# Mamba-2 block and ternary FFN on eight cores: the causal mask of the scan moves into PSUM, and three jobs leave VectorE

## The chip, the cores and the metric

The kernel runs on all 8 cores of one Trainium2 chip. Each core takes one half of the sequence of one of four batch rows. The cores don't wait for one another in the program. The metric is the device time in microseconds (us) of the slowest core.

## What is computed

The input has 4 rows of 2048 tokens with 2048 features. One layer is a Mamba-2 mixer and a feed-forward part with ternary weights, each with a residual and a LayerNorm. The core of the reference, shortened:

```
proj = hidden_states @ in_proj_w.T               # gate 4096, hbc 4352, dt 64
hbc = silu(conv4(hbc) + conv_b)                  # hs 4096, B 128, C 128
dt = softplus(dt + dt_bias);  A = -exp(A_log)    # 64 heads
step: state = state*exp(dt*A) + dt * x (outer) B;  y = state . C
y = (y + D*hs) * silu(gate);  y = rmsnorm(y) @ out_proj_w.T
x = layernorm(x + y)
x = layernorm(x + ffn(x))     # 8-bit rounded input, sign() weights, silu(g)*u, W_d
```

The kernel doesn't step through the tokens. For a tile of 128 tokens and a head with running sums a of dt*A it forms the matrix exp(a_t - a_s + ln dt_s) for all pairs of tokens s <= t, multiplies it by B_s.C_t, and multiplies that by x. What comes from earlier tiles is carried in a state of 128 x 4096.

## The kernel before

A small scheduler in Python (class `Prog`) takes the operations in the order in which they are written, puts each on the queue of its engine, and adds the semaphore waits that its lists of read and written names ask for. An engine runs its queue strictly in order, so the order of the code is the order of the work. The name of a buffer is the unit of a dependency: whoever writes `S32` waits for everybody who has read `S32` before. A dependency on an earlier operation of the same engine is a wait as well (except on TensorE).

The stages, with the places in the profiled span where they begin:

1. Projection and convolution of the previous half sequence, and its scan for the state at the end (`phase_a(False)`, `b1_pass`), from 0 us.
2. The same projection for the core's own 1024 tokens (`phase_a(True)`), and `scan_prep(True)`, which forms dt, a (`ahat`) and ln dt (`lndt`), and writes six arrays (high and low bf16 parts of a, -a and ln dt) to `flat_dram`, until about 1551 us.
3. The scan proper: a loop over 8 tiles `tt` of 128 tokens (lines 628 to 722), from 1600.7 to about 2720 us. This is where the change lies.
4. Output projection, LayerNorm, the FFN in two halves, the last LayerNorm.

A tile `tt` of the scan has these parts, in the order of the code:

- SyncE loads 8 panels of gate values into `sg_v` (L630). ScalarE applies Silu to all 4096 columns (L633, with a load of its function table before it). VectorE copies the state `S32` (f32, 4096 columns) to `Sbf` in bf16 (L635), so that the old state is there while the state is updated.
- `state_chunk` updates the state in 8 groups of 512 columns: L585, L594 and L596 on VectorE with matmuls L582, L588 and L591 between them. L596 writes `S32`.
- `g0rep`: one matmul for B_s.C_t (L637), which VectorE multiplies by the 0/1 mask `mask01` (L640), and three copies of the 128 columns beside it (L643), so that it serves four heads at once.
- 16 groups `hg` of four heads, in pairs. Each group: four matmuls with 6 rows each give the exponents of four heads (L650, `dmm`), VectorE cuts them off at 30 (L655, `dmin`), ScalarE takes the exponential (L657, `eexp`), VectorE multiplies by `g0rep` (L659, `ghat`), and four matmuls multiply by x (L664, `yi`). `dmatL` and `dmatR` hold the six rows.
- After the second group of a pair: the part of the old state (L671 from `Sbf`, L674), ScalarE brings one factor out of PSUM (L677, `eaev`), VectorE multiplies and adds (L678, L679 `yadd`), GpSimd has formed D*x in `hsd` (L680, `dhs`), VectorE adds it (L683, `yadd2`) and multiplies by the gate (L684, `ygate`), and ScalarE sums the squares (L687).
- RMSNorm, and the transposition of the tile by matmuls with the identity (L712, L719).

A pair thus handles 8 heads, and there are 8 pairs per tile and 64 in the scan. The groups share `DMIN` and are written one after the other; the matmuls of the second group stand behind `yi` of the first one on TensorE.

Of the kernel before, what the change touches and what calls it, by code (L numbers as in the profile page):

```python
# [174 lines left out]
def build_nc(taps=()):  # L175
    taps = set(taps)
    nc = bass.Bass("TRN2", target_bir_lowering=False)
    p = Prog()
# [38 lines left out]
    flat_dram = nc.dram_tensor("flat_dram", [NTT, 6, 64, 128], BF16, kind="Internal").ap()  # L217
# [22 lines left out]
    lndt = sb("lndt", [128, 512], F32)  # L240
# [25 lines left out]
    wsp = cv(AR5, 10240, 512, F32)  # L266
# [10 lines left out]
    y1 = cv(AR5, 12288, 512, F32)  # L277
    t_m = cv(AR5, 14336, 512, F32)
    ea_g = cv(AR5, 16384, 512, BF16)
    g0rep = cv(AR5, 17408, 512, BF16)  # L280
    ghat_v = [cv(AR5, 18432, 512, BF16), cv(AR5, 19456, 512, BF16)]
    dmin_v = cv(AR5, 20480, 512, F32)
# [37 lines left out]
    p.dma("sync", lambda g: g.dma_start(out=cumut[:], in_=cumut_d), ["d"], ["cumut"])  # L320
    p.dma("gpsimd", lambda g: g.dma_start(out=mask01[:], in_=cumut_d), ["d"], ["mask01"])
    p.dma("sync", lambda g: g.dma_start(out=selm[:], in_=selm_d), ["d"], ["selm"])
    p.dma("sync", lambda g: g.dma_start(out=convb_sb[:], in_=convb_d), ["d"], ["convb"])
# [163 lines left out]
    def scan_prep(full):  # L487
# [19 lines left out]
      p.v(lambda v: v.tensor_add(wsp[:], wsp[:], lndt[:]), ["wsp", "lndt"], ["wsp"])  # L507
      p.s(lambda s: s.activation(wsb_bf[:], wsp[:], AF.Exp), ["wsp"], ["wsb_bf"])
      p.s(lambda s: s.activation(lam_row[:], arow[:], AF.Exp), ["arow"], ["lam_row"])
      ea_tmp = cv(AR5, 8192, 512, BF16)  # L510
# [57 lines left out]
    def load_delta(tt):  # L568
        p.dma("sync", lambda g, tt=tt: g.dma_start(
            out=dmatL[0:2, :].rearrange("a (h t) -> a h t", h=64),  # L570
            in_=flat_dram[tt, 2:4]), [f"fl{tt}_2", f"fl{tt}_3", "dmatL"], ["dmatL"], tag="dlL")
        p.dma("sync", lambda g, tt=tt: g.dma_start(
            out=dmatL[4:6, :].rearrange("a (h t) -> a h t", h=64),
            in_=flat_dram[tt, 4:6]), [f"fl{tt}_4", f"fl{tt}_5", "dmatL"], ["dmatL"], tag="dlL")
        p.dma("sync", lambda g, tt=tt: g.dma_start(
            out=dmatR[2:4, :].rearrange("a (h t) -> a h t", h=64),
            in_=flat_dram[tt, 0:2]), [f"fl{tt}_0", f"fl{tt}_1", "dmatR"], ["dmatR"], tag="drL")

# [49 lines left out]
    for tt in range(NTT):  # L628
        for pan in range(8):
# [12 lines left out]
        for q in range(1, 4):  # L642
            p.v(lambda v, q=q: v.tensor_copy(g0rep[:, q * 128:(q + 1) * 128], g0rep[:, 0:128]),  # L643
                ["G0R"], ["G0R"], tag="g0rep")
        for hg in range(16):
            gb = hg % 2
            for j in range(4):
                h = hg * 4 + j
                p.t(lambda t, h=h, j=j, gb=gb:
                    t.matmul(pb[4 + gb][:, j * 128:(j + 1) * 128],  # L650
                             dmatL[0:6, h * 128:(h + 1) * 128],
                             dmatR[0:6, h * 128:(h + 1) * 128],
                             start=(j == 0), stop=(j == 3)),
                    ["dmatL", "dmatR"], [PB[4 + gb]], tag="dmm")
            p.v(lambda v, gb=gb: v.tensor_scalar_min(dmin_v[:], pb[4 + gb][:, :], 30.0),  # L655
                [PB[4 + gb], "DMIN"], ["DMIN"], tag="dmin")
            p.s(lambda s, gb=gb: s.activation(ghat_v[gb][:], dmin_v[:], AF.Exp),  # L657
                ["DMIN"], [f"GH{gb}"], tag="eexp")
            p.v(lambda v, gb=gb: v.tensor_mul(ghat_v[gb][:], ghat_v[gb][:], g0rep[:]),  # L659
# [9 lines left out]
            if hg % 2 == 1:  # L669
# [12 lines left out]
                       ["XT", "drep", "HSD"], ["HSD"], tag="dhs")  # L682
                p.v(lambda v: v.tensor_add(y1[:], y1[:], hsd[:]), ["y1", "HSD"], ["y1"], tag="yadd2")  # L683
                p.v(lambda v, g2=g_: v.tensor_mul(sg_v[:, g2 * 512:(g2 + 1) * 512], y1[:],  # L684
# [309 lines left out]
def _prep_shared(inputs):  # L994
# [23 lines left out]
    ident = np.eye(128, dtype=f32)  # L1018
    cumut = np.ascontiguousarray(np.triu(np.ones((128, 128), dtype=f32)))
    e01 = np.ascontiguousarray(np.kron(np.eye(64, dtype=f32), np.ones((1, 64), dtype=f32)))  # L1020
    return dict(wip=wip, convd=convd, convb=convb, wop=wop, wg=wg, wu=wu, wd=wd,
                dtb_t=dtb, alog_t=alog, d_row=drow, nw_t=nw_t,
                ident_in=ident, cumut_in=cumut, e01_in=e01)

# [34 lines left out]
```

How the kernel before makes its waits and increments, by code:

```python
            def run(eng):  # L158
                for op in per[ename]:
                    for (sk, v) in op.waits:
                        eng.wait_ge(sems[sk], v)
                    inst = op.fn(eng)
                    if op.milestone:
                        inst.then_inc(sems[op.semkey], 16 if op.is_dma else 1)
```

## Time and profile before

| | |
|---|---|
| median of 2 runs | 6089.91 us (6080.96 and 6098.87) |
| the profiled execution | 6059.51 us, span of its slowest core 6058.0 us |
| spans of the 8 cores in it | 5981.7 to 6058.0 us |
| granted TensorE clock, mean of a core | 0.761 to 0.767 of full speed |
| busy share of the span | TensorE 54%, VectorE 21%, ScalarE 16%, GpSimd 8% |
| scan (1600.7 to 2720 us) | TensorE busy 28%, VectorE 51%, ScalarE 19%, GpSimd 10% |

A time is in us from the first instruction of the core. Busy shares over the whole span mix stages with different limits, so the shares of the scan alone stand in the last line. In the rows, PE is TensorE, DVE is VectorE, ACT is ScalarE, POOL is GpSimd. AR stands for the arenas AR2 to AR5, in which most buffers lie, pb for a PSUM bank.

### The profile page before, as it was taken

How to read it: one execution, taken by the hardware profiler on the slowest of the kernel's cores; microseconds unless marked ns; L12 is line 12 of the kernel's file. 1: busy time of each engine (PE TensorE's matmuls, PEld its weight loads, DVE VectorE, ACT ScalarE, POOL GpSimd, SP SyncE). 2: the span in 40 equal slices, each digit the busy share in tenths (PEclk: the TensorE clock that was granted, in tenths of full speed). 3: DMA queues.
4: the chain of work that ended last, by engine and by line, in shares of the span. 5: the costliest groups of instructions: out<-in, count | busy, mean ns of one | idle time of the engine just before them, and what ended most of it. 6: DMA issues, size and time to landing. Idle time of an engine off the chain costs nothing.

```text
span 6058.0 us, 43938 instructions; the slowest of 8 cores (5981.7 to 6058.0 us)
## 1 busy us (share of the span) xinstructions
PE 3248.0 (54%) x15085; PEld 1332.9 (22%) x15085; DVE 1275.5 (21%) x2081; ACT 978.7 (16%) x1315; POOL 461.8 (8%) x620
## 2 busy tenths in 40 slices
PE   5884389884222222226541176767556767755540
PEld 2440034441011111112210032322222323322200
DVE  0114400111355555550006600000000000000003
ACT  1220011221011111110001122221112222111110
POOL 0000000000011110011110000001110000011100
PEclk9995589996555555558985588889888888888885
DMA  5530176440000000003332223332334233233323
GB/s 79 62 44 4 32 115 97 64 54 6 27 8 8 8 8 9 12 4 51 55 64 72 52 39 56 56 58 28 62 51 75 39 56 56 39 61 60 61 78 114
DMA packets 260287, 291.43 MB, mean 48 GB/s; under 512 B 52658, under 2 KB 237106, under 8 KB 257588
## 3 DMA queue, kind: packets, MB, share of 16 engines
q0 software_dynamic: 216096, 190.45, 23.7%
q1 hardware_dynamic: 43972, 98.17, 4.9%
q8 instruction: 125, 2.05, 0.1%
q14 instruction: 94, 0.77, 0.1%
HBM read 434.13 MB, written 44.83 MB: 79 GB/s over the span
## 4 chain that ended last, share of the span: by engine, by line
PE 43%; DMA 24%; DVE 16%; issue 8%; ACT 8%; DVEq 1%; SPq 0%; ACTq 0%; POOL 0%; POOLq 0%; another core or an unknown queue 0%
PE pb L410 8%; PE pb L874 7%; PE pb L869 7%; DMA AR<-wu 6%; DMA AR<-wd 6%; PE pb L899 5%; PE pb L380 4%; DMA AR<-wop 3%; DMA AR<-part_dram 3%; PE pb L741 2%; PE pb L421 2%; DMA AR<-wip 2%; DVE XT L719 1%; DVE AR L594 1%; DVE AR L585 1%
## 5 line engine op out<-in xcount | busy, mean ns | idle before, releaser
L869 PE MATMUL pb<-AR 128*128 128x512 bf16 x2048 | 813.7, 397 | 193.1 <-ACT AR L851 139.4
L874 PE MATMUL pb<-AR 128*128 128x512 bf16 x2048 | 812.6, 397 | 184.8 <-ACT AR L858 95.9
L899 PE MATMUL pb<-XT,AR 128*128 128x512 bf16 x2048 | 555.9, 426 | 409.6 <-ACT AR L895 328.6
L410 PE MATMUL pb<-AR 128*128 128x512 bf16 (+1 forms) x3264 | 511.4, 308 | 35.2 <-DMA AR<-wip 35.2
L899 PEld LDWEIGHTS pb<-XT,AR 128*128 128x128 bf16 x2048 | 205.8, 106 | 759.6 <-issue 610.2
L741 PE MATMUL pb<-AR,XT 128*128 128x512 bf16 x1024 | 258.2, 396 | 176.1 <-DMA AR<-wop 119.2
L880 DVE TENSOR_TENSOR XT<-pb,AR 128x512 bf16<-128x512 f32 x128 | 88.6, 692 | 1220.3 <-PE pb L869 1051.0
L410 PEld LDWEIGHTS pb<-AR 128*128 128x128 bf16 x3264 | 245.8, 97 | 299.1 <-issue 39.7
L664 PE MATMUL pb<-XT,AR 128*128 128x64 bf16 x512 | 47.6, 233 | 491.8 <-DVE AR L659 491.8
L869 PEld LDWEIGHTS pb<-AR 128*128 128x128 bf16 x2048 | 207.0, 101 | 463.5 <-issue 245.4
L874 PEld LDWEIGHTS pb<-AR 128*128 128x128 bf16 x2048 | 207.8, 101 | 458.8 <-issue 238.8
L452 DVE CAST XT<-pb 128x512 bf16<-128x512 f32 x128 | 88.5, 692 | 988.8 <-PE pb L447 971.1
L895 ACT ACTIVATE AR<-AR 128x512 bf16<-128x512 bf16 x256 | 160.8, 629 | 799.5 <-DMA AR<-wd 799.5
L380 PE MATMUL pb<-AR 128*128 128x512 bf16 x1024 | 223.2, 381 | 61.6 <-DMA AR<-wip 61.6
L588 PE MATMUL pb<-AR,BT 128*128 128x512 bf16 x128 | 75.0, 586 | 297.4 <-DVE AR L585 297.4
L878 ACT ACTIVATE AR<-pb 128x512 bf16<-128x512 f32 x128 | 76.4, 597 | 786.1 <-PE pb L869 786.1
L905 POOL DMA_DIRECT2D AR<-wd x240 | 126.8, 529 | 949.2 <-PE pb L899 891.0
L680 POOL TENSOR_TENSOR AR<-XT,AR 128x512 f32<-128x512 bf16 x64 | 115.7, 1808 | 1019.3 <-DVE AR L683 767.3
L416 ACT CAST AR<-pb 128x512 bf16<-128x512 f32 (+1 forms) x204 | 91.0, 446 | 537.1 <-PE pb L410 527.2
L741 PEld LDWEIGHTS pb<-AR,XT 128*128 128x128 bf16 x1024 | 95.0, 100 | 339.0 <-issue 255.0
L421 PE MATMUL pb<-AR 128*128 128x512 bf16 x544 | 130.1, 381 | 62.9 <-ACT AR L416 58.0
L664 PEld LDWEIGHTS pb<-XT,AR 128*128 128x128 bf16 x512 | 30.8, 117 | 522.1 <-issue 522.1
(194 smaller groups left out, 2931.6 us busy)
## 6 DMA issues: line engine op xcount, KB each, us to landing
AR<-wip POOLq DMA_DIRECT2D x26, 2048.0 KB, 19.2
AR<-wg POOLq DMA_DIRECT2D x32, 1024.0 KB, 13.9
AR<-wu POOLq DMA_DIRECT2D x32, 1024.0 KB, 20.3
AR<-wd POOLq DMA_DIRECT2D x256, 128.0 KB, 2.9
AR<-part_dram SPq DMA_DIRECT2D x48, 512.0 KB
AR<-wop POOLq DMA_DIRECT2D x128, 128.0 KB, 2.9
part_dram<-AR SPq DMA_DIRECT2D x32, 512.0 KB
AR<-convd POOLq DMA_DIRECT2D x68, 128.0 KB, 4.9
```

The lines of the kernel that those rows point to most:

```text
L380: t.matmul(pb[bank][:, :], x_fm_v[:, kc * TE + 3 + tt * 128: kc * TE + 3 + (tt + 1) * 128], wv[:, kc, :], start=(kc == 0), stop=(kc == NKC ...
L410: t.matmul(pb[bank][:, 0:j1 - j0], wv[:, kc, (oc - (pan - 8) * 4) * 128:(oc - (pan - 8) * 4 + 1) * 128], x_fm_v[:, kc * TE + j0: kc * TE + ...
L416: s.copy(hbc_v[:, slot * TE + j0: slot * TE + j1], pb[bank][:, 0:j1 - j0]),
L421: t.matmul(pb[bank][:, :], convd_v[cslot][:, k * 128:(k + 1) * 128], hbc_v[:, slot * TE + j0 + k: slot * TE + j0 + k + 512], start=(k == 0 ...
L680: p.pool(lambda g, tt=tt, g2=g_: g.tensor_mul(hsd[:], XT[:, tt * INTER + g2 * 512: tt * INTER + (g2 + 1) * 512], drep[:, g2 * 512:(g2 + 1) ...
L741: t.matmul(pb[tt][:, :], XT[:, tt * INTER + kc * 128: tt * INTER + (kc + 1) * 128], wopb[i][:], start=(kc == 0), stop=(kc == 31)),
L869: t.matmul(pb[jg][:, :], wgbr[:, kc, oc * 128:(oc + 1) * 128], xqTr[:, kc, jg * 512:(jg + 1) * 512], start=(kc == 0), stop=(kc == NKC - 1)),
L874: t.matmul(pb[2 + jg][:, :], wubr[:, kc, oc * 128:(oc + 1) * 128], xqTr[:, kc, jg * 512:(jg + 1) * 512], start=(kc == 0), stop=(kc == NKC ...
L880: p.v(lambda v, ho=ho, jg=jg: v.tensor_mul(p_fm[:, ho * T + jg * 512: ho * T + (jg + 1) * 512], pb[2 + jg][:, :], sgev[:]), [PB[2 + jg], " ...
L895: p.s(lambda s, i=i: s.sign(wdb[i][:], wdb[i][:]), [f"wdb{i}"], [f"wdb{i}"], tag="sgnD")
L899: t.matmul(pb[oc * 2 + jg][:, :], wdb[i][:, oc * 128:(oc + 1) * 128], p_fm[:, kci * T + jg * 512: kci * T + (jg + 1) * 512], start=(kci == ...
L905: p.dma("gpsimd", lambda g, opan=opan, Hhalf=Hhalf, nxt_k=nxt_k, i=i: g.dma_start(out=wdb[i][:], in_=wd_d[opan, Hhalf * 32 + nxt_k]), [f"w ...
```

## The change

It edits the scan at five places and adds two constants.

1. **The mask.** A fifth matmul is added to the PSUM bank of each group (`dmmtri`). It adds 30000 wherever s > t: `negid` is 30000 times the identity, and `slo4` is the strictly lower triangle of ones, four times side by side. The exponents are now formed with the opposite sign (the rows of `dmatL` and `dmatR` are loaded with a and -a exchanged, and `lndt` is negated in `scan_prep`), and ScalarE takes exp(-1 * value) straight out of PSUM. The cut at 30 on VectorE (`dmin`) goes.
2. **`Sbf`** is copied by ScalarE instead of VectorE, behind Silu of the gate.
3. **The three copies of `g0rep`** are made by ScalarE.
4. **`yadd2`**, the addition of D*x, is done by GpSimd.
5. **Constants**: two more DMAs on GpSimd's queue at the start (128 x 512 and 128 x 128, f32 in DRAM), and one small operation on VectorE in `scan_prep(True)`.

```diff
+    p.dma("gpsimd", lambda g: g.dma_start(out=slo4[:], in_=slo4_d), ["d"], ["slo4"])
+    p.dma("gpsimd", lambda g: g.dma_start(out=negid[:], in_=negid_d), ["d"], ["negid"])
...
+      if full:
+        p.v(lambda v: v.tensor_scalar(lndt[:], lndt[:], -1.0, None, ALU.mult),
+            ["lndt", "wsp"], ["lndt"], tag="negln")
...
-            in_=flat_dram[tt, 2:4]), [f"fl{tt}_2", f"fl{tt}_3", "dmatL"], ["dmatL"], tag="dlL")
+            in_=flat_dram[tt, 0:2]), [f"fl{tt}_0", f"fl{tt}_1", "dmatL"], ["dmatL"], tag="dlL")
...
-            in_=flat_dram[tt, 0:2]), [f"fl{tt}_0", f"fl{tt}_1", "dmatR"], ["dmatR"], tag="drL")
+            in_=flat_dram[tt, 2:4]), [f"fl{tt}_2", f"fl{tt}_3", "dmatR"], ["dmatR"], tag="drL")
...
-        p.v(lambda v: v.tensor_copy(Sbf[:], S32[:]), ["S32"], ["Sbf"], tag="sbf")
+        p.s(lambda s: s.copy(Sbf[:], S32[:]), ["S32"], ["Sbf"], tag="sbf")
...
-            p.v(lambda v, q=q: v.tensor_copy(g0rep[:, q * 128:(q + 1) * 128], g0rep[:, 0:128]),
+            p.s(lambda s, q=q: s.copy(g0rep[:, q * 128:(q + 1) * 128], g0rep[:, 0:128]),
...
-                             start=(j == 0), stop=(j == 3)),
+                             start=(j == 0), stop=False),
                     ["dmatL", "dmatR"], [PB[4 + gb]], tag="dmm")
-            p.v(lambda v, gb=gb: v.tensor_scalar_min(dmin_v[:], pb[4 + gb][:, :], 30.0),
-                [PB[4 + gb], "DMIN"], ["DMIN"], tag="dmin")
-            p.s(lambda s, gb=gb: s.activation(ghat_v[gb][:], dmin_v[:], AF.Exp),
-                ["DMIN"], [f"GH{gb}"], tag="eexp")
+            p.t(lambda t, gb=gb:
+                t.matmul(pb[4 + gb][:, :], negid[:], slo4[:], start=False, stop=True),
+                ["negid", "slo4"], [PB[4 + gb]], tag="dmmtri")
+            p.s(lambda s, gb=gb: s.activation(ghat_v[gb][:], pb[4 + gb][:, :], AF.Exp,
+                                              scale=-1.0),
+                [PB[4 + gb]], [f"GH{gb}"], tag="eexp")
...
-                p.v(lambda v: v.tensor_add(y1[:], y1[:], hsd[:]), ["y1", "HSD"], ["y1"], tag="yadd2")
+                p.pool(lambda g: g.tensor_add(y1[:], y1[:], hsd[:]), ["y1", "HSD"], ["y1"], tag="yadd2")
```

How the queues change is shown at three places. The line numbers of the changed kernel are larger by 2 to 11: L642 is Silu, L644 the copy to `Sbf`, L652 the `g0rep` copies, L659 `dmm`, L665 the mask matmul, L667 `eexp`, L670 `ghat`, L675 `yi`, L682 and L685 the matmuls of the old state, L688 `eaev`, L690 `yadd`, L691 `dhs`, L694 `yadd2`, L695 `ygate`, L698 the squares.

ScalarE at the start of the second tile, before:

```order
L633 ACTIVATE AR3<-AR3 128x4096 [waits sem_sync_d0,sem_sync_d1,sem_sync_d2,sem_sync_d3,sem_sync_d4,sem_sync_d5,sem_sync_d6,sem_sync_d7]
L657 ACTIVATE AR5<-AR5 128x512 [waits sem_vector] x2
L677 CAST AR5<-pb3 128x512 [waits sem_tensor]
L687 ACTIVATE AR5,sums8<-AR3 128x512 [waits sem_vector]
L657 ACTIVATE AR5<-AR5 128x512 [waits sem_vector] x2
```

ScalarE at the same place in the changed kernel:

```order
L642 ACTIVATE AR3<-AR3 128x4096 [waits sem_sync_d0,sem_sync_d1,sem_sync_d2,sem_sync_d3,sem_sync_d4,sem_sync_d5,sem_sync_d6,sem_sync_d7]
L644 CAST AR4<-AR4 128x4096
L652 COPY AR5<-AR5 128x128 [waits sem_vector]
L652 COPY AR5<-AR5 128x128 [waits sem_scalar] x2
L667 ACTIVATE AR5<-pb4 128x512 [waits sem_tensor]
L667 ACTIVATE AR5<-pb5 128x512 [waits sem_tensor]
L688 CAST AR5<-pb3 128x512 [waits sem_tensor]
L698 ACTIVATE AR5,sums8<-AR3 128x512 [waits sem_vector]
```

The copy L644 and the copies L652 now stand behind Silu and ahead of the first exponential, and the exponentials wait for TensorE instead of VectorE.

VectorE at the start of the second tile, before:

```order
L635 CAST AR4<-AR4 128x4096
L585 TENSOR_TENSOR AR4<-pb0,XT 128x512 [waits sem_tensor,sem_vector]
L594 TENSOR_TENSOR AR5<-AR4,pb2 128x512 [waits sem_tensor]
L596 TENSOR_TENSOR AR4<-AR5,pb1 128x512 [waits sem_vector]
L585 TENSOR_TENSOR AR4<-pb0,XT 128x512 [waits sem_tensor]
```

VectorE there in the changed kernel (the lines of `state_chunk` are larger by 9):

```order
L594 TENSOR_TENSOR AR4<-pb0,XT 128x512 [waits sem_tensor,sem_vector]
L603 TENSOR_TENSOR AR5<-AR4,pb2 128x512 [waits sem_tensor]
L605 TENSOR_TENSOR AR4<-AR5,pb1 128x512 [waits sem_scalar,sem_vector]
L594 TENSOR_TENSOR AR4<-pb0,XT 128x512 [waits sem_tensor]
L603 TENSOR_TENSOR AR5<-AR4,pb2 128x512 [waits sem_tensor,sem_vector]
```

The copy is gone from the head of the queue, and the first write of `S32` (L605) has a wait for ScalarE that it had not.

VectorE in the first pair of head groups of a tile, before:

```order
L655 TENSOR_SCALAR AR5<-pb4 128x512 [waits sem_tensor]
L659 TENSOR_TENSOR AR5<-AR5 128x512 [waits sem_scalar,sem_vector]
L655 TENSOR_SCALAR AR5<-pb5 128x512 [waits sem_tensor,sem_vector]
L659 TENSOR_TENSOR AR5<-AR5 128x512 [waits sem_scalar]
L678 TENSOR_TENSOR AR5<-pb7,AR5 128x512 [waits sem_scalar,sem_tensor]
L679 TENSOR_TENSOR AR5<-AR5,pb6 128x512 [waits sem_vector]
L683 TENSOR_TENSOR AR5<-AR5 128x512 [waits sem_gpsimd,sem_vector]
L684 TENSOR_TENSOR AR3<-AR5,AR3 128x512 [waits sem_vector]
```

VectorE there in the changed kernel:

```order
L670 TENSOR_TENSOR AR5<-AR5 128x512 [waits sem_scalar] x2
L689 TENSOR_TENSOR AR5<-pb7,AR5 128x512 [waits sem_scalar,sem_tensor]
L690 TENSOR_TENSOR AR5<-AR5,pb6 128x512 [waits sem_vector]
L695 TENSOR_TENSOR AR3<-AR5,AR3 128x512 [waits sem_gpsimd]
L670 TENSOR_TENSOR AR5<-AR5 128x512 [waits sem_scalar] x2
```

GpSimd's queue, which held only `dhs` (L680) in the scan, in the changed kernel:

```order
L691 TENSOR_TENSOR AR5<-XT,AR3 128x512 [waits sem_vector]
L694 TENSOR_TENSOR AR5<-AR5 128x512 [waits sem_gpsimd,sem_vector]
L691 TENSOR_TENSOR AR5<-XT,AR3 128x512 [waits sem_gpsimd]
L694 TENSOR_TENSOR AR5<-AR5 128x512 [waits sem_gpsimd,sem_vector]
L691 TENSOR_TENSOR AR5<-XT,AR3 128x512 [waits sem_gpsimd]
```

VectorE keeps five operations of a pair out of eight. `ygate` (L695) waits for GpSimd's addition (L694), and GpSimd's next `dhs` (L691) waits for the same addition.

TensorE in the first pair of the changed kernel; without the two L665 rows and with the old numbers it is the order of before:

```order
L659 MATMUL pb4<-AR2 128x128 x3
L665 MATMUL pb4<-slo4,negid 128x512
L675 MATMUL pb6<-XT,AR5 128x64 [waits sem_vector]
L675 MATMUL pb6<-XT,AR5 128x64 x3
L659 MATMUL pb5<-AR2 128x128 x4
L665 MATMUL pb5<-slo4,negid 128x512
```

## Rows read from the trace of the kernel before

**Rows 1.** Busy time by stage: PE, PEld, DVE, ACT, POOL; granted clock, DMA share, GB/s.
```profile
960.00:1340.00 380.00, 325.54 (x2022) 155.08 (x2020) 38.69 (x56) 85.53 (x156) 31.92 (x38) 1.00 0.48 65
1600.70:2720.00 1119.30, 314.56 (x1604) 122.64 (x1605) 572.25 (x1076) 211.52 (x360) 114.60 (x63) 0.50 0.03 8
```
**Rows 2.** The chain that ended last, in one pair: start us, us, what.
```profile
2364.40 0.70 DVE AR L683
```
**Rows 3.** One pair in time: start us, us, engine, line, operation [idle before <-releaser].
```profile
2354.75 0.69 DVE L684 TENSOR_TENSOR AR<-AR 128x512 bf16<-128x512 f32 x1
...
2355.54 0.63 ACT L687 ACTIVATE AR<-AR 128x512 f32<-128x512 bf16 x1 [3.34 <-DVE AR L684]
...
2356.17 0.61 ACT L657 ACTIVATE AR<-AR 128x512 bf16<-128x512 f32 x1
...
2357.76 0.60 PE L650 MATMUL pb<-AR 6*128 6x128 bf16 x4
2358.54 0.69 DVE L655 TENSOR_SCALAR AR<-pb 128x512 f32<-128x512 f32 x1 [1.23 <-PE pb L650]
2359.32 0.63 ACT L657 ACTIVATE AR<-AR 128x512 bf16<-128x512 f32 x1 [2.54 <-DVE AR L655]
2360.05 0.43 DVE L659 TENSOR_TENSOR AR<-AR 128x512 bf16<-128x512 bf16 x1 [0.82 <-ACT AR L657]
...
2360.81 0.61 PE L671 MATMUL pb<-AR,C_fm 128*128 128x512 bf16 x1
2361.36 0.60 PE L674 MATMUL pb<-AR,ea_fm 64*128 64x512 bf16 x1
...
2362.05 0.59 ACT L677 CAST AR<-pb 128x512 bf16<-128x512 f32 x1 [2.10 <-PE pb L674]
...
2363.61 0.69 DVE L679 TENSOR_TENSOR AR<-AR,pb 128x512 f32<-128x512 f32 x1
2364.40 0.69 DVE L683 TENSOR_TENSOR AR<-AR 128x512 f32<-128x512 f32 x1
2365.19 0.69 DVE L684 TENSOR_TENSOR AR<-AR 128x512 bf16<-128x512 f32 x1
2365.23 1.67 POOL L680 TENSOR_TENSOR AR<-XT,AR 128x512 f32<-128x512 bf16 x1 [8.78 <-DVE AR L683]
```
**Rows 4.** The start of a later tile in time.
```profile
2301.56 2.28 DVE L635 CAST AR<-AR 128x4096 bf16<-128x4096 f32 x1
2301.79 3.06 POOL L680 TENSOR_TENSOR AR<-XT,AR 128x512 f32<-128x512 bf16 x1 [33.17 <-DVE XT L719]
...
2303.69 3.62 ACT L633 ACTIVATE AR<-AR 128x4096 bf16<-128x4096 bf16 x1
...
2306.61 0.69 DVE L596 TENSOR_TENSOR AR<-AR,pb 128x512 f32<-128x512 f32 x1
```
**Rows 5.** The start of the first tile in time.
```profile
1605.02 3.62 ACT L633 ACTIVATE AR<-AR 128x4096 bf16<-128x4096 bf16 x1
...
1605.82 0.69 DVE L596 TENSOR_TENSOR AR<-AR,pb 128x512 f32<-128x512 f32 x1
```
**Rows 6.** From the mask product to the first exponential of a tile, in time.
```profile
2331.89 0.28 DVE L640 TENSOR_TENSOR AR<-pb,mask 128x128 bf16<-128x128 f32 x1
...
2333.91 1.28 ACT L657 ACT_TABLE_LOAD   x1 [26.60 <-DVE AR L655]
```
**Rows 7.** A short ScalarE operation, in time.
```profile
1858.45 0.29 ACT L694 ACTIVATE stat<-stat,eps 128x1 f32<-128x1 f32 x1 [0.62 <-DVE stat L692]
```
**Rows 8.** GpSimd's line L680 in the whole run: shortest, median, longest in ns.
```profile
L680 POOL TENSOR_TENSOR AR<-XT,AR x64: 1144/1663/3066, 1573.5 to 2687.8; 128x512 f32<-128x512 bf16 x64
```
**Rows 9.** The start of the program, in time.
```profile
2.75 0.53 POOL L348 DMA_DIRECT2D drw<-d_row  x1
...
51.36 9.01 PE L410 MATMUL pb<-AR 128*128 128x512 bf16 x48 [35.22 <-DMA AR<-wip]
```
**Rows 10.** Eight matmuls of 512 columns in the first stage of rows 1, in time.
```profile
1323.13 1.89 PE L421 MATMUL pb<-AR 128*128 128x512 bf16 x8 [0.85 <-ACT AR L416]
```

More of the change, by code:

```diff
@@ L205, in build_nc @@
     e01_d = di("e01_in", [64, INTER])
+    slo4_d = di("slo4_in", [128, 512])
+    negid_d = di("negid_in", [128, 128])
     out_d = nc.dram_tensor("out", [HID, T], F32, kind="ExternalOutput").ap()
@@ L222, in build_nc @@
     ident = sb("ident", [128, 128], BF16)
+    slo4 = sb("slo4", [128, 512], BF16)
+    negid = sb("negid", [128, 128], BF16)
     cumut = sb("cumut", [128, 128], F32)
@@ L1019, in _prep_shared @@
     cumut = np.ascontiguousarray(np.triu(np.ones((128, 128), dtype=f32)))
+    slo4 = np.ascontiguousarray(np.tile(
+        (np.arange(128)[:, None] > np.arange(128)[None, :]).astype(f32), (1, 4)))
+    negid = np.ascontiguousarray(30000.0 * np.eye(128, dtype=f32))
     e01 = np.ascontiguousarray(np.kron(np.eye(64, dtype=f32), np.ones((1, 64), dtype=f32)))
@@ L1022, in _prep_shared @@
                 dtb_t=dtb, alog_t=alog, d_row=drow, nw_t=nw_t,
-                ident_in=ident, cumut_in=cumut, e01_in=e01)
+                ident_in=ident, cumut_in=cumut, e01_in=e01,
+                slo4_in=slo4, negid_in=negid)
 def make_in_maps(inputs):
```

## The prediction

> **What bounds the kernel now.** I read the busy time by stage first. In the scan, 1119.3 us long, no engine is near full: VectorE is busy for 572 us, TensorE for 315, ScalarE for 212 and GpSimd for 115, and the granted clock is 0.50, the lower level, 1.2 GHz [rows 1]. A stage in which the busiest engine is busy for half of the time is bounded by waits, so what counts is the chain and not the load. The chain that ended last runs through every operation of a pair of head groups, VectorE's addition L683 among them [rows 2]. The timeline shows why: a pair takes 10.44 us, from `ygate` at 2354.75 to `ygate` at 2365.19, and in it each operation begins about 0.1 us after the one that it needs has ended [rows 3]. The 64 pairs are 668 us of the scan. Only two things lie beside the chain: GpSimd's `dhs`, and the `dmm` matmuls of a pair's first group, which are issued before `eaev`. So an operation taken off VectorE gains nothing by making VectorE freer; it gains or loses by what takes its place in the chain.
>
> **The pair, step by step.** Starts are from [rows 3].
> - First group. Before, from `ygate` (2354.75) the exponential (2356.17) is reached in 1.42 us. `dmin` stands in between, but so do the squares L687 (2355.54), which ScalarE does first in its queue, and the exponential starts 0.63 us after them. The squares stay. Removing `dmin` here uncovers them: no gain. The mask matmul of this group is issued behind `dmm` and is over before ScalarE is free: it is hidden by the chain `eaev` to `ygate`, more than 3 us. Cost 0.
> - Second group. Before, `dmm` at 2357.76 to the exponential at 2359.32: 1.56 us. Now the mask matmul follows the four `dmm`. These are 512 columns together, and the 512 columns of L671 hold up L674 for 0.55 us (2360.81 to 2361.36); the four `dmm` are over after 0.60 with one of them still ending, so 0.40 is the least. I take 0.50. From the start of a 512-column matmul to ScalarE's start on its result is 0.69 (L674 at 2361.36, L677 at 2362.05). Sum 1.19 instead of 1.56: 0.37 us gained, between 0.32 and 0.47.
> - `yadd2`. Before, `yadd` (2363.61) to `ygate` (2365.19) takes 1.58 us. Now GpSimd starts 0.83 after `yadd`, as L680 starts 0.83 after L683 (2364.40 to 2365.23), then comes its addition, then 0.10 until VectorE starts (the exponential of 0.63 us at 2359.32 is followed by `ghat` 0.73 later). No row shows an addition of two f32 tiles on GpSimd. The nearest is its own multiplication L680 of the same 512 columns: 1144 ns at its shortest, 1663 in the median, 3066 at the longest [rows 8]. The shortest is the first one, when VectorE did nothing; the longest began under the 2.28 us copy L635 and ended 1.01 us after it (2303.84 to 2304.85) [rows 4]; and the usual one begins 0.04 us after `ygate` and ends 1.02 us after it [rows 3]. So L680 needs about 1.1 us and stands still while VectorE works on two SBUF operands or on the long copy. VectorE waits during the new addition, so I take 1.14. Bounds: VectorE's own 0.69 below, the 3.06 above. Sum 0.83 + 1.14 + 0.10 = 2.07 instead of 1.58: 0.49 us lost, between 0.04 and 2.4.
> - All else in the pair is unchanged. Net 0.12 us lost per pair, times 64: 8 us.
>
> **The start of a tile.** Before, the copy to `Sbf` takes VectorE 2.28 us and `S32` is first written by L596 at 2306.61 [rows 4]. Now the copy stands behind Silu on ScalarE, which waits for the gate panels, and ends at 2303.69 + 3.62 = 2307.31. ScalarE reads an f32 tile of 512 in the time of a bf16 one (0.63 for both, L657 and L687 [rows 3]), so the copy of 4096 takes as long as Silu, 3.62 us, and ends at 2310.93. L596 waits for it and starts at 2311.0, 4.4 us late, and all of VectorE's queue stands behind it: the next L585, and with that TensorE. What VectorE saves, 2.28 us, is spent waiting. In the first tile Silu starts at 1605.02, since the state and the gates are loaded late; L596 goes from 1605.82 to 1605.02 + 3.62 + 3.62 + 0.10 = 1612.36, 6.5 us late [rows 5]. Sum 7 x 4.4 + 6.5 = 37 us. Bounds for the copy: 2.28 us as on VectorE, or eight times 0.63, 5.0 us: 11 us less or more in all. This is the largest term.
>
> **The `g0rep` copies.** From L640 to the table load ahead of the first exponential takes 2.02 us [rows 6]. Now: 0.38 until ScalarE can begin (0.28 + 0.10), then three copies. A ScalarE operation of one column takes 0.29 [rows 7] and one of 512 takes 0.63; I take 0.30 for 128 columns and 0.10 for each wait on the one before. 0.38 + 3 x 0.40 = 1.58, since `dmin` is gone too. 0.4 us gained per tile, 3 us in all, and 5 us lost if each copy takes 0.63. The table load stays behind the copies.
>
> **The rest.** Two DMAs are issued ahead of the loads for the first projection, at 0.53 us each, and bring 0.33 MB beside the 12.6 MB (of f32, by the shapes) that arrive before the first big matmul at 51.36 [rows 9]: 1.1 us and 1.2 us, 2 us together, between 0 and 3. The negation of `lndt` runs on VectorE while TensorE and ScalarE work for it: 0.
>
> **Sum.** 37 + 8 - 3 + 2 = 44 us more. On the profiled execution of 6059.5 us that is 6103.5. The median of the runs shown, 6089.9, is 30 above the profiled execution, and the measurement will be made as that one was: 6134 us, 0.7% more. About 2%, 122 us, is what a measurement of this kernel can tell from no change.
>
> **Rival 1: `dhs` takes the port ahead of `ygate`.** The end of GpSimd's addition releases both `ygate` and the next `dhs`. Before, both were released by VectorE, `ygate` began 0.04 us earlier and kept its 0.69 us, while `dhs` was stretched [rows 3]. If `dhs` is first now, `ygate`, whose two operands lie in SBUF, would stand still for the rest of it, about 1.0 us (1.14 less the start), in each pair. 64 us more: 6198. For it: the event now comes from GpSimd itself. Against it: GpSimd began later than VectorE after the same event in every pair seen. The Trainium skill ("SBUF — State Buffer", "Who interferes with whom") states the rule: a VectorE instruction with two SBUF inputs contends with a GpSimd one that reads SBUF, and whichever issues first blocks the other fully. The stretched `dhs` agrees for the one order; the other order is not in this trace. By that rule the sum is 6134 or 6198 and nothing between.
>
> **Rival 2: slower, since the addition itself is slow.** Place: L694 in the new chain between `yadd` and `ygate`, where nothing covers it. Each 0.1 us costs 6.4 us. The 2% are reached at 1.14 + (122 - 44) / 64 = 2.36 us, or, if rival 1 holds as well, at 1.36 us. With the longest duration seen, 3.06 us, the time is 6134 + 64 x 1.92 = 6257. For it: both inputs and the output are f32, and the multiplication reads bf16. Against it: its time fits a cost per element, and VectorE takes 0.69 for f32 and for mixed tiles alike.
>
> **Rival 3: the clock rises.** More matmul columns in the scan could lift the granted clock from 0.50 to the 1.00 of the dense stage [rows 1], where 512 columns take 1.89 / 8 = 0.24 us [rows 10] instead of 0.55. The chain of a pair holds five times 512 columns, at most 1.5 us, and a state group two, 0.6 us: 64 x 2.1 = 134 us less, 6000. Against it: TensorE is busy for 28% of the scan and would be for about 34%, with waits in each pair, and the clock is 0.50 for the whole of it.
>
> **The chances.** The forecast, 6100 to 6165, gets 0.62: its largest term rests on two durations that the trace shows. Rival 1 gets 0.20, rival 2 0.10, rival 3 0.03. The remaining 0.05 is for something that I don't see. The range from 6085 to 6210 holds the forecast with its copy bounds and rival 1, and leaves out rivals 2 and 3. Slower by over 2%: rival 2 and a part of rival 1 with it, 0.13. Faster by over 2%: 0.02, since even a free addition in GpSimd would give back only 64 x 1.14 = 73 us. Within 2%: 0.85.
>
> **What would show it.** In the trace of the changed kernel: the first state update of a tile waits for ScalarE's copy for about 4 us, and the copy takes 3.6 us; GpSimd's addition takes 1.1 to 1.2 us; `ygate` keeps 0.69 us, or about 1.7 under rival 1; a pair takes 10.5 to 10.6 us; the exponential of the second group starts 1.2 us after its `dmm`. The scan is 41 to 43 us longer, and the stages behind it keep their lengths. I am wrong if the update doesn't wait, if the addition takes over 1.4 us, or if the clock in the scan leaves 0.50.

## The result and the profile after

| | before | after |
|---|---|---|
| median of the runs taken side by side | 6064.94 us (10 runs) | 6127.03 us (11 runs) |
| ratio, 95% interval | | 1.0114 [1.0064, 1.0163] |
| profiled execution | 6059.5 us | 6121.1 us (span of the slowest core 6119.6) |
| mean span of the 8 cores | 6025.7 us | 6088.4 us |
| the scan, first update of `S32` to last `ygate` (slowest core) | 1092.3 us | 1137.4 us |

Some executions of each kernel show a lower granted clock on some of the cores and take up to 5% longer; the medians include them, the ratios don't, and of the profiles only that of e10 is of such an execution.

The kernel is 1.1% slower, which is within the 2%. The forecast was 6134 us (a ratio of 1.007). Between the two profiled executions the mean span of the cores grows by 62.7 us: 10.7 of them come before the first update of `S32` in the scan, 45.2 inside the scan, and 6.8 behind it.

The scan's window of the changed kernel, with the columns of [rows 1]:

```profile
1600.70:2720.00 1119.30, 368.96 (x1654) 129.63 (x1654) 401.76 (x799) 235.76 (x377) 174.66 (x122) 0.50 0.03 8
```

VectorE has 170 us less work in this window than in [rows 1]. A part of that is only shifted: the changed kernel is not through its scan when the window ends. Counted on each kernel from its first update of `S32` to its last `ygate`, VectorE is busy for 409 us instead of 556, 147 less, and for 36% of the time. The scan is longer all the same, and the clock is still 0.50. So VectorE's load was not the limit.

A pair of head groups in the changed kernel, from one `ygate` (L695) to the next, as [rows 3]:

```profile
2379.37 0.69 DVE L695 TENSOR_TENSOR AR<-AR 128x512 bf16<-128x512 f32 x1 [1.51 <-POOL AR L694]
2379.41 1.66 POOL L691 TENSOR_TENSOR AR<-XT,AR 128x512 f32<-128x512 bf16 x1
2380.15 0.63 ACT L698 ACTIVATE AR<-AR 128x512 f32<-128x512 bf16 x1 [3.95 <-DVE AR L695]
2380.78 0.58 ACT L667 ACTIVATE AR<-pb 128x512 bf16<-128x512 f32 x1
...
2382.34 0.60 PE L659 MATMUL pb<-AR 6*128 6x128 bf16 x4
2382.87 0.61 PE L665 MATMUL pb<-slo,negid 128*128 128x512 bf16 x1
2383.57 0.60 ACT L667 ACTIVATE AR<-pb 128x512 bf16<-128x512 f32 x1 [2.21 <-PE pb L665]
...
2387.89 0.69 DVE L690 TENSOR_TENSOR AR<-AR,pb 128x512 f32<-128x512 f32 x1
2388.72 1.26 POOL L694 TENSOR_TENSOR AR<-AR 128x512 f32<-128x512 f32 x1 [7.66 <-DVE AR L690]
2390.09 0.69 DVE L695 TENSOR_TENSOR AR<-AR 128x512 bf16<-128x512 f32 x1 [1.51 <-POOL AR L694]
```

The pair takes 10.72 us; the mean of a tile is 10.72 to 10.86, against 10.44 to 10.49 before. The exponential of the second group comes 1.23 us after its `dmm` (1.56 before): the mask in PSUM gains 0.33. From `yadd` (L690) to `ygate` takes 2.20 us (1.58 before): the detour over GpSimd loses 0.62. VectorE's note at `ygate` names what it stood idle for, GpSimd's L694. `dhs` (L691) starts 0.04 us behind `ygate`, as before, and is the one that is stretched. That holds for all 56 pairs that another pair of the same tile follows, on all eight cores.

The start of a tile, the second, as [rows 4]:

```profile
2333.34 0.69 DVE L594 TENSOR_TENSOR AR<-pb,XT 128x512 bf16<-128x512 f32 x1
2333.53 1.28 ACT L642 ACT_TABLE_LOAD   x1 [22.22 <-DMA AR<-gate_dram]
2334.82 3.62 ACT L642 ACTIVATE AR<-AR 128x4096 bf16<-128x4096 bf16 x1
2335.41 0.69 DVE L603 TENSOR_TENSOR AR<-AR,pb 128x512 f32<-128x512 f32 x1 [1.37 <-PE pb L600]
2338.34 3.59 ACT L644 CAST AR<-AR 128x4096 bf16<-128x4096 f32 x1
2342.10 0.69 DVE L605 TENSOR_TENSOR AR<-AR,pb 128x512 f32<-128x512 f32 x1 [6.01 <-ACT AR L644]
```

VectorE stands idle for 6.01 us until the copy L644 is over. From the last `ygate` of a tile to the first update of the next takes 33.2 to 34.0 us, against 29.2 to 29.6.

The way from `g0` (L649) to the first exponential, as [rows 6]:

```profile
2367.36 0.28 DVE L649 TENSOR_TENSOR AR<-pb,mask 128x128 bf16<-128x128 f32 x1
2367.73 1.06 ACT L652 COPY AR<-AR 128x128 bf16<-128x128 bf16 x3 [25.80 <-DVE AR L649]
2368.81 1.28 ACT L667 ACT_TABLE_LOAD   x1
2370.11 0.60 ACT L667 ACTIVATE AR<-pb 128x512 bf16<-128x512 f32 x1
```

The table load begins 1.45 us after L649. From L649 to the first `ghat` takes 3.45 us, against 3.95.

And the instructions that the sum was made of (count, ns of the shortest, median and longest, first and last start):

```profile
L644 ACT CAST AR<-AR x8: 3587/3588/3589, 1605.8 to 2630.5; 128x4096 bf16<-128x4096 f32 x8
L694 POOL TENSOR_TENSOR AR<-AR x64: 1259/1259/1262, 1646.1 to 2745.6; 128x512 f32<-128x512 f32 x64
L695 DVE TENSOR_TENSOR AR<-AR x64: 691/693/693, 1647.5 to 2747.0; 128x512 bf16<-128x512 f32 x64
L652 ACT COPY AR<-AR x24: 297/298/298, 1635.9 to 2661.0; 128x128 bf16<-128x128 bf16 x24
```

### The profile page after: what moved, and what is told of

The parts are those of the page before. It is cut to its first block, busy times and chain, and to the rows that moved or that the text cites. A ratio compares the mean times of both kernels' runs of the same rounds, so it can differ in the third digit from the quotient of the medians.

```text
span 6119.6 us, 44015 instructions; the slowest of 8 cores (6035.9 to 6119.6 us)
## 1 busy us (share of the span) xinstructions
PE 3324.7 (54%) x15213; PEld 1346.2 (22%) x15213; DVE 1126.6 (18%) x1858; ACT 1009.5 (16%) x1347; POOL 530.0 (9%) x686
## 4 chain that ended last, share of the span: by engine, by line
PE 43%; DMA 24%; DVE 14%; issue 8%; ACT 8%; POOL 2%; DVEq 1%; SPq 0%; ACTq 0%; POOLq 0%; another core or an unknown queue 0%
PE pb L416 8%; PE pb L885 7%; PE pb L880 7%; DMA AR<-wu 7%; DMA AR<-wd 6%; PE pb L910 5%; PE pb L386 4%; DMA AR<-wop 3%; DMA AR<-part_dram 3%; PE pb L752 2%; PE pb L427 2%; DMA AR<-wip 1%; DVE AR L603 1%; DMA flat_dram<-AR 1%; DVE AR L594 1%
## 5 line engine op out<-in xcount | busy, mean ns | idle before, releaser
L910 PEld LDWEIGHTS pb<-XT,AR 128*128 128x128 bf16 x2048 | 202.9, 105 | 762.5 <-issue 613.1
L675 PE MATMUL pb<-XT,AR 128*128 128x64 bf16 x512 | 47.6, 233 | 432.3 <-DVE AR L670 432.3
L852 POOL DMA_DIRECT2D AR<-wg x32 | 28.1, 878 | 1451.5 <-PE pb L880 1024.7
L694 POOL TENSOR_TENSOR AR<-AR 128x512 f32<-128x512 f32 x64 | 80.6, 1260 | 811.5 <-DVE AR L690 811.5
```

The costliest lines, as they stand in the source:

```text
L910: t.matmul(pb[oc * 2 + jg][:, :], wdb[i][:, oc * 128:(oc + 1) * 128], p_fm[:, kci * T + jg * 512: kci * T + (jg + 1) * 512], start=(kci == ...
```

## The experiments

The theory was that the chain alone sets the scan, so that each part of the change has its own price and the prices add up. The rival was that some of it comes from load, contention or the matmuls. For each kernel I read the same stretches: one pair, the last `ygate` to the next tile's first update, `g0` to the first `ghat`, and the scan from first update to last `ygate`. The columns are of the slowest core: the mean of the pairs, the mean of the tile starts, the median of `g0` to `ghat`. The diffs are against the changed kernel, with cuts marked by dots.

| kernel | ratio to before [95%] | pair | tile start | `g0` to `ghat` | scan |
|---|---|---|---|---|---|
| before | 1 | 10.47 | 29.4 | 3.95 | 1092.3 |
| after | 1.0114 [1.0064, 1.0163] | 10.77 | 33.5 | 3.45 | 1137.4 |
| e1_sbf_first | 1.0017 [1.0003, 1.0030] | 10.77 | 27.4 | 3.45 | 1094.7 |
| e2_yadd2_dve | none | 10.08 | 33.4 | 3.45 | 1093.3 |
| e3_mask_only | 0.9923 [0.9897, 0.9950] | 10.12 | 29.4 | 1.87 | 1054.0 |
| e4_two_hsd | 1.0169 [1.0149, 1.0189] | 11.62 | 33.5 | 3.45 | 1185.4 |
| e11_g0rep_dve | 1.0066 [1.0029, 1.0103] | 10.77 | 33.4 | 1.87 | 1123.9 |
| e6_good_parts | 0.9936 [0.9904, 0.9968] | 10.12 | 27.4 | 1.87 | 1039.7 |

**e1_sbf_first: the same copy, on the same engine, one place earlier.**

```diff
+        p.s(lambda s: s.copy(Sbf[:], S32[:]), ["S32"], ["Sbf"], tag="sbf")
...
-        p.s(lambda s: s.copy(Sbf[:], S32[:]), ["S32"], ["Sbf"], tag="sbf")
```

The line moves from behind Silu to ahead of it.

> The changed kernel with the copy to Sbf written ahead of Silu of the gate, so that ScalarE makes it while it waits for the gate panels. My theory (the copy costs by its place in ScalarE's queue): the first state update of a tile no longer waits for ScalarE; from the last ygate of a tile to the first update of the next it takes about 27 us instead of 33.5 (29.4 in the kernel before), because the 2.28 us copy is gone from VectorE and nothing replaces it; 45 to 55 us less than the changed kernel in all, 10 us or less from the kernel before. Rival (moving a 4096-column copy from a 2.28 us engine to a 3.6 us one costs the difference wherever it stands): still 1.3 us per tile slower than before, 40 us above it.

Second tile, timeline of e1_sbf_first:

```profile
2275.14 3.59 ACT L642 CAST AR<-AR 128x4096 bf16<-128x4096 f32 x1
...
2297.54 1.28 ACT L643 ACT_TABLE_LOAD   x1 [18.82 <-DMA AR<-gate_dram]
...
2300.11 0.69 DVE L605 TENSOR_TENSOR AR<-AR,pb 128x512 f32<-128x512 f32 x1
```

The copy runs 25 us before the first update, while ScalarE has nothing else to do, and L605 no longer waits for it. The tile start falls by 6.1 us, to 2 below that of before: the 2.28 us copy on VectorE is saved as well. The place in the queue, not the engine, was the loss. The scan is 42.7 us shorter than in the changed kernel, and the time is 0.2% above that of before.

**e2_yadd2_dve: the addition back on VectorE.**

```diff
-                p.pool(lambda g: g.tensor_add(y1[:], y1[:], hsd[:]), ["y1", "HSD"], ["y1"], tag="yadd2")
+                p.v(lambda v: v.tensor_add(y1[:], y1[:], hsd[:]), ["y1", "HSD"], ["y1"], tag="yadd2")
```

> The changed kernel with yadd2 back on VectorE, all else as changed. My theory: a pair goes from 10.77 us back to 10.15 (yadd to ygate 1.58 instead of 2.20), 64 x 0.62 = 40 us less than the changed kernel, about 10 us above the kernel before. Rival (the 11 us that the first stages lost and the 7 us behind the scan are the real cost and the pair is harmless): less than 15 us gained.

Timeline of e2_yadd2_dve, `yadd` to `ygate`, all on VectorE:

```profile
2395.78 0.69 DVE L690 TENSOR_TENSOR AR<-AR,pb 128x512 f32<-128x512 f32 x1
2396.57 0.69 DVE L694 TENSOR_TENSOR AR<-AR 128x512 f32<-128x512 f32 x1
2397.36 0.69 DVE L695 TENSOR_TENSOR AR<-AR 128x512 bf16<-128x512 f32 x1
```

It has too few executions for a ratio, so its time shows nothing here. The trace has what was asked: 0.69 us less per pair and 44 less in the scan. Of the 0.69, 0.62 are the step from `yadd` to `ygate`. The other 0.07 lie at `minter` (L689): it starts 0.76 us after `eaev` here and in the kernel before, and 0.83 after it wherever `yadd2` is on GpSimd; why, no trace shows. And 10.08 against 10.47 of before is the price of the mask in a pair, 0.39 us gained.

**e3_mask_only: the mask alone.** The kernel before with the mask in PSUM; `Sbf`, `g0rep` and `yadd2` stay on VectorE.

```diff
-        p.s(lambda s: s.copy(Sbf[:], S32[:]), ["S32"], ["Sbf"], tag="sbf")
+        p.v(lambda v: v.tensor_copy(Sbf[:], S32[:]), ["S32"], ["Sbf"], tag="sbf")
...
-            p.s(lambda s, q=q: s.copy(g0rep[:, q * 128:(q + 1) * 128], g0rep[:, 0:128]),
+            p.v(lambda v, q=q: v.tensor_copy(g0rep[:, q * 128:(q + 1) * 128], g0rep[:, 0:128]),
...
-                p.pool(lambda g: g.tensor_add(y1[:], y1[:], hsd[:]), ["y1", "HSD"], ["y1"], tag="yadd2")
+                p.v(lambda v: v.tensor_add(y1[:], y1[:], hsd[:]), ["y1", "HSD"], ["y1"], tag="yadd2")
```

> The kernel before with the mask in PSUM alone (the mask matmul, the opposite signs, no dmin, the two constants); the copies and yadd2 stay on VectorE. My theory: the second group gains 0.32 us and the first one nothing, a pair takes 10.15 us instead of 10.47, 20 us less than the kernel before (0.3%), within its noise. Rival A (taking dmin off VectorE saves its 0.69 us in both groups): a pair takes 9.1 us, 88 us less. Rival B (the additional 512 columns cost what they last): pair 10.5 or more, no gain.

It gained 38 us in the scan, where I had expected 20, and 0.8% of the time. I had missed the part that the third stretch shows, 3.95 to 1.87. Timeline of e3_mask_only, second tile:

```profile
2303.21 0.61 PE L665 MATMUL pb<-slo,negid 128*128 128x512 bf16 x1
2303.49 0.69 DVE L605 TENSOR_TENSOR AR<-AR,pb 128x512 f32<-128x512 f32 x1
2303.89 1.28 ACT L667 ACT_TABLE_LOAD   x1 [24.84 <-PE pb L665]
2304.09 0.28 DVE L649 TENSOR_TENSOR AR<-pb,mask 128x128 bf16<-128x128 f32 x1
...
2305.19 0.60 ACT L667 ACTIVATE AR<-pb 128x512 bf16<-128x512 f32 x1
2305.96 0.43 DVE L670 TENSOR_TENSOR AR<-AR 128x512 bf16<-128x512 bf16 x1 [0.69 <-ACT AR L667]
```

The load of the exponential's table starts 0.20 us before L649, and in before it started 2.02 us after L640. It comes as soon as the wait of its exponential is met. That wait used to be for `dmin`, which stood in VectorE's queue behind the `g0rep` copies; now it is for the mask matmul, which ends at 2303.82, before L649 has begun.

**e11_g0rep_dve: only the `g0rep` copies back on VectorE** (the second pair of lines of the diff above). If that is right, the copies on ScalarE hold the table load back.

> The changed kernel with nothing but the g0rep copies back on VectorE. My theory, formed on the mask-only run: without dmin the first exponential of a tile waits for nothing that is late, so ScalarE loads its function table and takes that exponential while VectorE is still in the state updates; the copies on ScalarE put both behind the g0 product again. So the g0 product to first ghat falls from 3.45 to 1.9 us, 8 x 1.6 = 13 us less. Rival (what I predicted: the copies gain 0.4 us per tile on ScalarE): 3.85 us, 3 us more.

The theory held: 1.58 us less per tile, 13.5 in the scan. Timeline of e11_g0rep_dve, second tile:

```profile
2361.16 1.28 ACT L667 ACT_TABLE_LOAD   x1 [25.26 <-PE pb L665]
2361.35 0.28 DVE L649 TENSOR_TENSOR AR<-pb,mask 128x128 bf16<-128x128 f32 x1
2361.74 0.79 DVE L652 COPY AR<-AR 128x128 bf16<-128x128 bf16 x3
```

The table load stands ahead of L649, and the three copies on VectorE run beside it. The whole time went to a ratio of 1.0066, from 1.0114, but the two intervals overlap, so the gain rests on the trace.

**e4_two_hsd: rival 1 made to happen.** `hsd` gets two buffers, so `dhs` waits no longer for the addition but starts right behind it in GpSimd's own queue, before `ygate`.

```diff
-    hsd = cv(AR5, 0, 512, F32)
+    hsd2 = [cv(AR5, 0, 512, F32), cv(AR5, 20480, 512, F32)]
```

> The changed kernel with two buffers for D*x in turn, so that GpSimd's next dhs has no wait behind its own addition and starts at once, ahead of ygate. It removes a dependency and adds no work. My theory with the port rule of my rival 1: dhs gets ahead of ygate, ygate stands still until dhs has ended and shows about 1.6 us instead of 0.69 (or starts about 1 us later), a pair takes 11.7 us instead of 10.77, 55 to 65 us slower than the changed kernel. Rival (VectorE takes the port whenever it asks, whatever came first): ygate keeps 0.69, dhs is stretched, the pair stays at 10.77.

Timeline of one pair, and below it both lines over the scan, of e4_two_hsd:

```profile
2416.90 1.26 POOL L694 TENSOR_TENSOR AR<-AR 128x512 f32<-128x512 f32 x1 [9.22 <-DVE AR L690]
2418.12 1.15 POOL L691 TENSOR_TENSOR AR<-XT,AR 128x512 f32<-128x512 bf16 x1
2418.26 1.55 DVE L695 TENSOR_TENSOR AR<-AR 128x512 bf16<-128x512 f32 x1 [1.51 <-POOL AR L694]
```

```profile
L695 DVE TENSOR_TENSOR AR<-AR x64: 692/1551/1552, 1644.7 to 2792.2; 128x512 bf16<-128x512 f32 x64
L691 POOL TENSOR_TENSOR AR<-XT,AR x64: 1143/1149/1152, 1569.7 to 2780.4; 128x512 f32<-128x512 bf16 x64
```

Now `dhs` keeps 1.15 us and `ygate` grows from 0.69 to 1.55: each pair is 0.86 longer, and the scan 48, where I had expected 55 to 65. The rule of the Trainium skill ("SBUF — State Buffer", "Who interferes with whom"), that whoever issues first blocks the other fully, agrees for this order too, but for 0.15 us: `dhs` ends 1.01 us after `ygate` has begun, so a full stop would make `ygate` 1.01 + 0.69 = 1.70 us long. In the other order the same sum is 0.65 + 1.15 = 1.80 for `dhs`, and 1.66 is what it takes. Here a wait fewer made the scan slower. In the changed kernel the shared buffer was what kept `ygate` first.

**e6_good_parts: the parts that gain, together.** The mask, and the copy to `Sbf` ahead of Silu; `g0rep` and `yadd2` on VectorE.

> The changed kernel with the three costs of its trace undone: the copy to Sbf ahead of Silu on ScalarE, and yadd2 and the g0rep copies back on VectorE. Left of the change are the mask in PSUM and the early copy. My theory (all effects are shifts of one chain and add up): pair 10.1 us, last ygate to first update 27.3 to 27.6, g0 product to first ghat 1.9; against the kernel before 64 x 0.33 + 8 x (2.1 + 2.0) = 54 us less, about 0.9%. Rival (the gain of the mask-only kernel beyond 38 us was luck, and the parts overlap): less than 35 us.

The scan lost 52.7 us against before: 64 x 0.33 + 7 x 2.0 + 8 x 2.1 = 52. The prices add up, so the rival by load is gone. The time fell by 0.6%, no more than e3's within the intervals, though the scan is 14 us shorter than e3's. In the two profiled executions the stages behind the scan, whose code is the same, took 17 us longer in e6 (3336.7 us against 3319.7, mean of the cores), and that hides the 14.

**e7_pipe_mask: a direct test of "waits, not load".** The engines' work is that of e6, but the loop over pairs is written so that `dmm`, mask, exponentials and the matmuls of the old state of the next pair are issued ahead of the additions of this one.

```diff
-        for hg in range(16):
+        def head(hg):
...
+        head(0)
+        head(1)
+        inter(0)
+        for g_ in range(8):
+            p.v(lambda v: v.tensor_mul(t_m[:], pb[7][:, :], ea_g[:]), [PB[7], "ea_g"], ["t_m"], tag="minter")
...
+            if g_ < 7:
+                inter(g_ + 1)
+                head(2 * g_ + 2)
+                head(2 * g_ + 3)
+            p.v(lambda v: v.tensor_add(y1[:], t_m[:], pb[6][:, :]), ["t_m", PB[6]], ["y1"], tag="yadd")
```

> The same parts as in the kernel with the good parts, and the pairs written so that the chain is cut: the matmuls of the old state, dmm, the mask matmul and the exponentials of the next pair are issued ahead of the additions of this one. No work is added or left out. My theory (the scan waits, no engine is full): a pair is then bounded by VectorE's six operations and one wait for yi, 4.7 to 5.0 us instead of 10.1; 64 x 5.2 = 330 us less than the kernel before, with the other parts 5 to 6%. Rival (ScalarE or TensorE at the low clock takes over): 6 us per pair or more.

Timeline (`ygate` is L706, `minter` L684), and the busy time of a window inside the scan, of e7_pipe_mask:

```profile
2102.80 0.69 DVE L706 TENSOR_TENSOR AR<-AR 128x512 bf16<-128x512 f32 x1
...
2107.70 0.69 DVE L706 TENSOR_TENSOR AR<-AR 128x512 bf16<-128x512 f32 x1
2108.31 0.68 DVE L684 TENSOR_TENSOR AR<-pb,AR 128x512 f32<-128x512 f32 x1
```

```profile
1600.00:2280.00 680.00, 345.53 (x1537) 120.41 (x1537) 434.02 (x846) 211.50 (x325) 89.52 (x56) 0.50 0.04 13
```

A pair takes 4.9 us instead of 10.1 with the same operations at the same clock, and the scan 722 us instead of the 1040 of e6. The ratio is 0.9419 [0.9248, 0.9591]. VectorE is now busy for 64% of the window.

**e8_pipe_dmin and e9_pipe_pool: do the two parts of the change count once the order is good?** e8 is e7 with `dmin` and the old signs back (two `dmin` buffers); e9 is e7 with `yadd2` on GpSimd.

> The pipelined kernel with dmin on VectorE instead of the mask in PSUM (two DMIN buffers). If VectorE is what bounds a pair once the chain is cut, the two dmin cost what they last, 2 x 0.79 us: pair 6.3 to 6.6, 100 us slower than the pipelined kernel with the mask, where the same step was worth 21 us in the chain. Rival (they are hidden beside TensorE): pair as in the pipelined kernel with the mask, within 0.3 us.

> The pipelined kernel with yadd2 on GpSimd. My theory: VectorE's queue is in order, ygate still waits for GpSimd and what VectorE could do meanwhile stands behind it, so the 0.62 us of the detour are paid here too: pair 5.5 us instead of 4.9, 35 to 40 us slower than the pipelined kernel. Rival (with the chain cut, VectorE bounds the pair and an operation less on it is a gain): pair 4.9 or less.

e8: 0.9483 [0.9442, 0.9524]; a pair takes 5.44 us, and from the first to the last `ygate` is 735.1 us against 690.0 in e7. I had expected 100, and it is 45: 30 in the pairs, 0.54 us each where two `dmin` last 1.3, and 15 between `g0` and the first `ghat` of a tile (5.56 us instead of 3.44). So part of the two `dmin` goes into stretches in which VectorE waited. The ratios of e7 and e8 can't be told apart. e9: 0.9392 [0.9350, 0.9434], not to be told from e7 by the ratio; by the trace a pair takes 5.21 us and the stretch 711.1, 21 more than e7's where I expected 35 to 40. GpSimd's detour still stands in the chain, at half its price or less.

**e10_pipe_all: the state updates too.** e7, with `state_chunk` pipelined in the same manner (`XW` tracked per group, the next group's product and matmul ahead of this group's update).

```diff
-                [PB[0], "XT"], ["XW"], tag=f"{phase}xw")
+                [PB[0], "XT"], [f"XW{g_}"], tag=f"{phase}xw")
...
+            if g_ < 7:
+                lx(g_ + 1)
+                xw(g_ + 1)
```

> The pipelined kernel with the state updates written in the same way in both scans (the matmuls and the XW product of the next group ahead of the update of this one). A group of 512 columns takes 3.52 us now, of which VectorE works 2.06. Theory: 2.3 to 2.5 us per group, bounded by VectorE; 128 groups, 130 to 150 us less than the pipelined kernel, 8% less than the kernel before. Rival (TensorE at the low clock bounds the group, three matmuls of 0.53 us each with their waits): 3 us per group, half of that gain.

The ratio is 0.9062 [0.9035, 0.9088]. Timeline of core 5 of e10_pipe_all (mean granted clock 0.79; not the slowest core):

```profile
1912.90 0.68 DVE L619 TENSOR_TENSOR AR<-AR,pb 128x512 f32<-128x512 f32 x1
1913.68 0.69 DVE L614 TENSOR_TENSOR AR<-AR,pb 128x512 f32<-128x512 f32 x1
1914.29 0.68 DVE L596 TENSOR_TENSOR AR<-pb,XT 128x512 bf16<-128x512 f32 x1
1914.89 0.68 DVE L619 TENSOR_TENSOR AR<-AR,pb 128x512 f32<-128x512 f32 x1
```

The three VectorE operations of a state group stand one behind the other: 1.99 us a group instead of 3.52, and less than the 2.3 to 2.5 that I had expected. For 128 groups that makes about 196 us, where I had expected 130 to 150; the time is 9.4% below the kernel before, where I had expected 8.

## Why the prediction was right, and where its terms were off

The kernel slowed down by the mechanism that was forecast: work that moved to other engines changed the chain, and not the load. That 6127 lies within 7 us of 6134 is in part luck, since two misses cancel. The median of the kernel before came out at 6064.9 us and not at 6089.9, 25 lower; and the change cost more than the forecast 44 us: 62 by the medians, 63 by the mean span, 69 by the ratio (39 to 99 by its interval, which holds 44 as well). Each term:

- **The start of a tile, 4.4 us: measured 4.2.** The copy took 3.59 us where 3.62 was taken from Silu, and L605 waited for it. e1 shows it to be the whole loss. Seven tiles make 29 us, where the forecast had 31.
- **The first tile, 6.5: measured 7.0. The start DMAs, 2: about 1, within the spread.** Together with the rest of the start they are 10.7 (mean over the cores of the first update's start). The first update of the scan starts 7.28 us after the first Silu on every core, with the copy in between, and before it started 0.3 after it in the mean (0.8 on the core of [rows 5]): 7.0. The other 3.7 are a later Silu, 1602.6 against 1598.9 in the mean. The six kernels e1, e2, e3, e4, e6 and e11 have the same two DMAs at the start and begin Silu at 1598.3 to 1600.9, 1599.7 in the mean, so most of the 3.7 is the spread from execution to execution.
- **The second group's mask, 0.37 gained: right.** The step itself gained 0.33, since the mask matmul starts 0.53 us after `dmm` where 0.50 was taken; the whole pair gained 0.39 (e2 and before) or 0.35 (e3 and before).
- **The first group, 0: right,** the squares are ahead of it (2380.15) and the exponential follows them.
- **`yadd2`, 0.49 lost: mis-sized, it is 0.62 in the step and 0.69 in the pair.** The addition of two f32 tiles takes 1.26 us, not the 1.14 of the multiplication that reads bf16, and `minter` starts 0.07 later, which the sum had not foreseen. The pair thus lost 0.30 us and not 0.12, and 64 of them 19 us and not 8. Rival 2 had the right place but not the size: it needed 2.36 us.
- **The `g0rep` copies, 0.4 gained per tile: 0.5 measured, and yet the step was not understood.** "The table load stays behind the copies" is true of the changed kernel, but I took the copies on ScalarE for a part of the gain. e3 and e11 show that the mask alone frees 2.1 us per tile and that the copies on ScalarE take 1.6 of it back. A net result near the forecast hid two larger ones. (The bound for copies of 0.63 us each, 5 us lost, is 4.4 by its own numbers.)
- **Rival 1 did not happen:** `ygate` began 0.04 us before `dhs` in every pair in which both were released together, and kept 0.69 (0.691 to 0.693 in all 64). e4 shows that the mechanism is real; its price is 0.86 us, where I had 1.0.
- **Rival 3 did not happen:** 0.50 in the scan, with TensorE busy for 33% of it, and also in e7 with 51%.
- **The stages behind the scan, 0:** they are 7 us longer in the mean of eight cores. But e1, e2, e3, e4, e6 and e11 have the same code there as the changed kernel, and in their profiled executions these stages take 3317.5 to 3336.7 us in the mean of the cores, against 3334.4 before and 3341.2 after. These executions of one and the same code are up to 24 us apart, so no run shows that the 7 us are a cost of the change.

By part, in the scan, from the experiments: the mask -38 us (e3), the `g0rep` copies +13.5 (e11), `yadd2` +44 (e2), `Sbf` +29 (7 x 4.2). That is +48, and +45 was measured. The forecast's "41 to 43" counts the first tile's 6.5, which lies ahead of this stretch; without it, the forecast for the same stretch is 35: -27 for the mask and the copies together (-24.5 measured), +31 for `yadd2` (+44), +31 for `Sbf` (+29). So one term was off, `yadd2`, by 13 us: 8 by the longer addition, which no row had shown, and 4 by the later `minter`.

## What to carry to other kernels

In a stage where no engine is near full, read the chain and its order, not the busy time: taking 147 us of work off VectorE made the kernel slower, and the pipelined order took 5.8% (e7) and 9.4% (e10) off the time of the kernel before, of which the mask and the early copy are 0.6% (e6). When an operation goes to an idle engine, look at what stands ahead of it in that queue and whether it needs to: one line moved ahead of Silu was worth 6 us a tile. When a wait goes, look for a second instruction that its wait had kept in place, above all a table load or a GpSimd operation beside a VectorE one; and measure each part alone before a near-zero sum is believed.

## What the runs showed of the hardware

- The activation table load stands behind the wait of the activation that needs it, not behind the previous activation alone. By what that activation waits for, its 1.28 us stand whole behind `g0` or begin before it (e11 against the changed kernel: 1.87 against 3.45 us from `g0` to `ghat`). In e3 they are still not free: VectorE is idle for 0.69 us ahead of the first `ghat`.
- On 512 columns, GpSimd took 1.26 us for an f32 addition and 1.14 for a multiplication of bf16 tiles with an f32 result. The Trainium skill ("GPSIMD Engine Reference", "Performance versus the Vector engine") gives one rate for two-input operations, some 2.6 cycles per element; here the two differ by a tenth.
- The exclusion between VectorE and GpSimd works both ways: 0.69 becomes 1.55 us for VectorE if GpSimd is 0.14 us ahead (e4), and 1.14 becomes 1.66 for GpSimd if VectorE is 0.04 ahead. The one that is second loses about 0.15 us less than the time for which the other still runs.
- ScalarE copied 128 x 4096 from f32 to bf16 in 3.59 us, VectorE in 2.28; where ScalarE is idle, the longer copy is the cheaper one (e1).
